# Expert and slot numbers held as bytes, and one register load for a round of eight tiles, in a two-layer tower on one core

## The chip, the cores and the metric

One NeuronCore of a Trainium2 chip runs the whole program. The metric is the device time of one execution in microseconds (us). Three executions of the kernel before are at hand. The engines are called as the profile calls them: PE (TensorE; PEld is its weight load), DVE (VectorE), ACT (ScalarE), POOL (GpSimd) and SP (SyncE, which issues DMAs). Each has its own sequencer, which goes through that engine's instructions in order and hands the work to the engine.

## The reference

The program is a tower of two layers over 8 x 500 tokens of width 128: embeddings, a state-space layer and a mixture of experts, then sparse attention and a second mixture of experts. The change touches only how the two mixtures find their weights. Per token and expert they compute

```
h = jax.nn.relu(xf @ W1e + b1e)
y = h @ W2e + b2e
acc = acc + cwe[:, None] * y        # cwe is zero but for the token's chosen experts
```

The first mixture has 8 experts with 512 hidden units and picks 2 of them per token. The second has 64 experts (8 groups of 8) with 256 hidden units and picks 4 per token.

## The kernel before

For each mixture f (0 and 1) the kernel sorts the token rows by expert, cuts the sorted rows into blocks of 128 and goes through *tiles*: a tile is one block with one expert that has rows in it. There are 70 tiles in loop 0 and 252 in loop 1, the most that the sorting can need, and the loops are written out: PE, DVE, ACT, POOL and SP each have a straight list of instructions in rounds of RING = 8 tiles. Which expert a tile belongs to, and which block, depends on the data, so it stands in tables that DVE writes (L1148 to L1170) and the sequencers of PE and DVE read into registers.

One tile works as follows, in the order of each engine's list:

- PE (`expert_tensor`, its inner `tiles` at L660): while blocks still come in, it turns the next block (L633, one matmul record). `first(u + 1, ...)` multiplies the next tile's block by W1 (L638, 8 records in loop 0, 4 in loop 1); the block's place in the ring of turned blocks comes from a register. `second(..., u)` multiplies the hidden values of this tile by W2 (L645, 8 records or 4); where the expert's W2 begins comes from a register. It waits for DVE's and ACT's part of the hidden values (L673, L674), and for W1 and the block of the next tile.
- DVE (`expert_vector`, its inner `tiles` at L579): copies the turned block out of PSUM (L554), does half of bias and relu (L559), and copies W1 of the tile three ahead from `big` into a ring of four (`stage`, L550); where W1 begins comes from a register. In loop 1, from tile 148 on, it adds one gathered result on three of four tiles (`combine_pick`, L1328).
- ACT does the other half of bias and relu (L605) and copies the results (L623). SP stores results, two tiles in one DMA.
- POOL gathers the sorted rows of each block with an indirect DMA (L867, 63 blocks in loop 0 and 126 in loop 1, in a ring of eight), and in loop 1 later gathers results (L874).

The registers are held by the class `Words` (L469). It has two words a tile for eight tiles, of which DVE uses the first. Four registers are filled by one register load (L478, TENSOR_LOAD in the trace): two tiles at a time, always for the same tiles of the *next* round, after every second tile:

```
second(words.value(u, 0), u)
if u % 2 and first_tile + u + RING < c.tiles:
    words.load(first_tile + RING, u - 1)
```

Before a loop, `Words` issues four such loads (L475), which fill the first eight tiles, on PE ahead of its first turn, and on DVE ahead of its first stage; DVE has one more for tiles 1 and 2 (`pairs_of`, L461). `value` (L481) reads a register into an address: FUSED_REGOPS in the trace, one instruction that holds several register operations; on PE `second` has another one for each further piece of W2 (L645). The tables hold 32-bit words that are already multiplied: (expert x columns of W1 or W2) and (place in the ring x 128). They are written by one-partition operations of DVE once per mixture: L1164 and L1165 the experts, L1166 and L1167 the places for DVE, L1169 and L1170 the places for PE.

Of the kernel before, what the change touches and what calls it, by code (L numbers as in the profile page):

```python
# [18 lines left out]
I32 = mybir.dt.int32  # L19
I16 = mybir.dt.int16  # L20
U32 = mybir.dt.uint32
ALU = mybir.AluOpType
# [3 lines left out]
D = 128  # L26
# [18 lines left out]
class Ffn:  # L45
# [25 lines left out]
    def blocks_for(self, tile):  # L71
# [15 lines left out]
TAB = FFN[1].tab  # L87
# [6 lines left out]
KEEP = {0: 32, 1: 67}  # L94
# [63 lines left out]
def tower_kernel(nc, a, out):  # L158
# [15 lines left out]
    with ExitStack() as ctx:  # L174
# [7 lines left out]
        def sb(name, shape, dt=F32):  # L182
            return ctx.enter_context(nc.sbuf_tensor(name, shape, dt))
# [78 lines left out]
        table = sb("table", [1, 2 * TAB], I32)  # L262
        w0 = 2 * FFN[0].tab
        assert 2 * w0 <= 2 * TAB <= 512
        tile_tables = [table[0:1, 0:w0], cst[0:1, 128:128 + 2 * TAB].bitcast(I32)]
        stage_tables = [table[0:1, w0:2 * w0], table[0:1, 0:2 * TAB]]
# [192 lines left out]
        def pairs_of(engine, table, tau, n, top_a, top_b):  # L459

            _, words = nc.values_load_multi_w_load_instructions(  # L461
                table[0:1, bass.ds(tau * 2, 2 * n)], engines=[engine], min_val=0, max_val=max(top_a, top_b),
                skip_runtime_bounds_check_because="the tables hold clipped numbers of experts and places in the ring")

            def within(word, top):
                return nc.s_assert_within(word, 0, top, skip_runtime_bounds_check_because="the tables hold clipped numbers")
            return [within(w, top_a) for w in words[0::2]], [within(w, top_b) for w in words[1::2]]

        class Words:  # L469

            def __init__(self, engine, p, table, first, top_a, top_b):
                self.engine, self.table, self.first, self.tops = engine, table, first, (top_a, top_b)
                self.regs = [engine.alloc_register(f"{p}word{n}") for n in range(2 * RING)]
                for u in range(0, RING, 2):
                    self.load(0, u)  # L475

            def load(self, first_tile, u):
                self.engine.reg_load(self.regs[2 * u:2 * u + 4], self.table[0:1, bass.ds((first_tile + (self.first + u)) * 2, 4)])  # L478

            def value(self, u, which):  # L480
                word = self.engine.snap(self.regs[2 * u + which], min_val=0, max_val=max(self.tops))  # L481
                return nc.s_assert_within(word, 0, self.tops[which], skip_runtime_bounds_check_because="the tables hold clipped numbers")
# [59 lines left out]
        def expert_vector(dve, c, combine_pick):  # L542
# [6 lines left out]
            def stage(w1, u):  # L549
                v.tensor_copy(ring.w1[u % U], w1v[:, bass.ds(w1, c.wcols)]).then_inc(S(p + "w1_ready"), 1)  # L550
# [15 lines left out]
            w1, _ = pairs_of(mybir.EngineType.DVE, stage_tables[c.n], 0, 2, (c.E - 1) * c.wcols, (KEEP[c.n] - 1) * 128)  # L566
            words = Words(dve, p, stage_tables[c.n], 2, (c.E - 1) * c.wcols, (KEEP[c.n] - 1) * 128)
# [4 lines left out]
            stage(w1[0], 1)  # L572
            dve.wait_ge(S(p + "turned"), 2)
            v.tensor_copy(ring.blocks[:, 128:256], ps[:, 1, 0:128]).then_inc(S(p + "blocks_in"), 1)
            stage(w1[1], 2)
# [3 lines left out]
            def tiles(first_tile, count):  # L579
                for u in range(count):  # L580
                    if first_tile + u in c.turn_at:
                        n = c.turn_at[first_tile + u]
                        dve.wait_ge(S(p + "turned"), n + 1)
                        turn(n)
                    dve.wait_ge(S(p + "hid_filled"), first_tile + (u + 4))
                    rectify(u + 1)
                    stage(words.value(u, 0), u + 3)
                    if u % 2 and first_tile + u + RING < c.tiles:
                        words.load(first_tile + RING, u - 1)
                    n = first_tile + u - COMBINE_AT  # L590
                    if c.n and n >= 0 and n % COMBINE_STEP:
                        combine_pick(n - n // COMBINE_STEP - 1)
# [35 lines left out]
        def expert_tensor(pe, c):  # L628
# [20 lines left out]
            words = Words(pe, p, tile_tables[c.n], 0, (c.E - 1) * c.HC * D, (KEEP[c.n] - 1) * 128)  # L649
# [295 lines left out]
        def _(dve):  # L945
# [45 lines left out]
            def route(c, me, dve):  # L991
# [162 lines left out]
                keep = KEEP[f]  # L1154
                numbers = tileno[0:1, 0:tab]
                tiles_, stages_ = (t_.rearrange("o (t w) -> o t w", w=2) for t_ in (tile_tables[f], stage_tables[f]))
                if f:
                    me.did(TT(out=block, in0=numbers, in1=one, op=ALU.subtract))
# [3 lines left out]
                else:  # L1162
                    me.did(TT(out=block, in0=numbers, in1=one, op=ALU.subtract))
# [1136 lines left out]
```

## Time and profile before

| | |
|---|---|
| three executions | 1136.02, 1134.34, 1134.40 us; median 1134.4 |
| profiled execution, first to last instruction (span) | 1221.9 us |
| profiled execution's own time | the profile gives no other than its span |
| loop 0 in the span | 257.7 to 393 us |
| loop 1 in the span | 793.1 to 1142 us |
| instructions recorded | 18019 |

A row of the trace gives the start in us from the beginning of the span, the duration, the engine, the line of the kernel and the operation. An engine with a q behind its name (PEldq, DVEq) is that engine's sequencer. The profiled execution is 87.5 us longer than the median.

### The profile page before, as it was taken

The page shows a single profiled execution, that of the slowest core. Times are in us where ns is not written, and L with a number is a line of the kernel's source. Part 1 is how long each engine was busy: PE and PEld are TensorE (multiplying, and loading weights), DVE is VectorE, ACT ScalarE, POOL GpSimd, SP SyncE. Part 2 cuts the span into 40 slices and gives each one's busy share as a digit, 9 for nine tenths or more (in the row PEclk, how much of TensorE's full clock was granted, in tenths as well). Part 3 has the DMA queues.
Part 4 walks back from the last instruction along what each step waited for, and adds up shares of the span by engine and source line. Part 5 has one row for each costly group of instructions (what it writes and reads, how often), then busy time and mean ns, then how long its engine had stood idle before and what let it go on. Part 6 is the DMA issues. An engine that isn't in the chain of part 4 may idle for free.

```text
span 1221.9 us, 18019 instructions
## 1 busy us (share of the span) xinstructions
PE 802.4 (66%) x5133; PEld 637.8 (52%) x5133; DVE 778.2 (64%) x2305; ACT 437.9 (36%) x1233; POOL 510.6 (42%) x528
## 2 busy tenths in 40 slices
PE   0218963879998248778587511287887897888343
PEld 0105552679998124434255401177776787777332
DVE  7885467656665248888766699855555555666642
ACT  2543241524444134443103304533343444444200
POOL 7841001255540634662101002466664435555574
PEclk9759965579999556666665555599999998999755
DMA  2290089012221287566400404133332223333222
GB/s 69 76 403 37 1 249 309 1 50 70 71 66 38 60 143 140 118 143 131 77 1 1 132 0 127 33 85 85 89 83 81 83 77 87 88 96 94 59 72 75
DMA packets 116599, 112.95 MB, mean 92 GB/s; under 512 B 16403, under 2 KB 102994, under 8 KB 116258
## 3 DMA queue, kind: packets, MB, share of 16 engines
q1 hardware_dynamic: 103228, 84.68, 25.3%
q0 software_dynamic: 13280, 27.13, 8.2%
q8 instruction: 49, 0.80, 0.3%
q14 instruction: 42, 0.34, 0.1%
HBM read 76.15 MB, written 35.57 MB: 91 GB/s over the span
## 4 chain that ended last, share of the span: by engine, by line
PE 55%; DVE 22%; issue 9%; POOL 5%; ACT 4%; DMA 3%; another core or an unknown queue 1%; SPq 0%; DVEq 0%; POOLq 0%; ACTq 0%
PE ps L638 18%; PE ps L645 15%; DVE wide L1348 6%; PE ps L1969 4%; POOL wide L810 3%; PE ps L633 3%; DVE wide L1229 3%; PE ps L2231 3%; PE ps L2139 2%; PE ps L2180 2%; ACT wide L1757 2%; DVE bnst L955 2%; POOL wide L874 1%; PE ps L2076 1%; PE ps L2224 1%
## 5 line engine op out<-in xcount | busy, mean ns | idle before, releaser
L645 PE MATMUL ps<-big,wide 128*128 x1568 | 238.1, 282 | 33.9 <-ACT wide L605 20.6
L638 PE MATMUL ps<-wide 128*128 (+1 forms) x1580 | 247.1, 287 | 18.9 <-DVE wide L554 12.2
L867 POOL DMA_INDIRECT wide<-xrows,holder x189 | 182.8, 967 | 158.1 <-PE ps L633 116.1
L559 DVE TENSOR_SCALAR wide<-ps,wide 128x128 f32<-128x128 f32 x395 | 131.7, 348 | 156.9 <-PE ps L638 138.4
L638 PEld LDWEIGHTS ps<-wide 128*128 128x128 f32 x1580 | 206.2, 195 | 40.8 <-issue 32.9
L645 PEld LDWEIGHTS ps<-big,wide 128*128 128x128 f32 x1568 | 203.7, 194 | 44.5 <-issue 43.9
L605 ACT ACTIVATE wide<-ps,wide 128x128 f32<-128x128 f32 x395 | 137.8, 367 | 202.4 <-PE ps L638 184.9
L1348 DVE TENSOR_REDUCE wide<-ps 125x3 f32<-125x1500 f32 (+1 forms) x96 | 143.7, 1540 | 46.7 <-PE ps L1969 45.3
L874 POOL DMA_INDIRECT wide<-results,place x128 | 127.6, 997 | 100.1 <-DVE h L1328 44.0
L1969 PE MATMUL ps<-big 97*125 97x500 bf16 x256 | 104.8, 545 | 40.3 <-DVE wide L1348 32.5
L623 ACT COPY wide<-ps 128x128 f32<-128x128 f32 x322 | 85.2, 264 | 92.1 <-PE ps L645 78.1
L550 DVE COPY wide<-big 128x258 f32 (+2 forms) x328 | 107.4, 327 | 3.9 <-issue 3.8
L856 POOL TENSOR_SCALAR wide<-tileno,sm 125x128 f16<-125x128 f16 x36 | 23.5, 653 | 172.2 <-DVE sm L1210 143.0
L1969 PEld LDWEIGHTS ps<-big 97*125 97x125 bf16 x256 | 42.6, 191 | 89.5 <-DVE wide L1348 50.8
L901 POOL DMA_INDIRECT wide<-results,place x64 | 60.9, 952 | 60.4 <-SPq L540 34.3
L554 DVE COPY wide<-ps 128x128 f32<-128x128 f32 x185 | 53.7, 290 | 41.5 <-PE ps L633 33.5
L1328 DVE SCALAR_TENSOR_TENSOR h<-wide,gate,h 125x128 f32<-125x128 f32 x128 | 43.2, 350 | 28.7 <-DMA wide<-results,place 23.4
L2248 PE MATMUL ps<-wide 125*128 125x79 f16 (+2 forms) x192 | 22.1, 262 | 54.6 <-DVE wide L1229 49.7
L633 PE MATMUL ps<-cst,wide 128*128 128x128 f32 x189 | 53.7, 287 | 5.5 <-issue 5.2
L1757 ACT ACTIVATE wide<-h,shift,rs 125x128 f32<-125x128 f32 x112 | 45.2, 483 | 25.6 <-DVE shift L972 19.4
L2119 PE MATMUL ps<-cst,wide 125*128 125x125 f32 x96 | 20.9, 370 | 48.6 <-ACT wide L1757 48.4
L2231 PE MATMUL ps<-b,cst 8*125 8x128 f32 (+1 forms) x128 | 33.0, 435 | 24.8 <-issue 20.6
(388 smaller groups left out, 1102.7 us busy)
## 6 DMA issues: line engine op xcount, KB each, us to landing
results<-wide SPq DMA_DIRECT2D x161, 128.0 KB, 1.8
big<-kappa SPq DMA_DIRECT2D x8, 1750.0 KB, 21.0
big<-parts SPq DMA_DIRECT2D x96, 125.0 KB
big<-in_L_ffn_W_dram SPq DMA_DIRECT2D x10, 1024.0 KB, 9.4
big<-in_L_ffn_W_dram SPq DMA_DIRECT2D x64, 128.0 KB, 2.6
parts<-wide SPq DMA_DIRECT2D x24, 250.0 KB
xrows<-wide SPq DMA_DIRECT2D x2, 1792.0 KB
wide<-results,place POOLq DMA_INDIRECT x192
```

The lines of the kernel that those rows point to most:

```text
L550: v.tensor_copy(ring.w1[u % U], w1v[:, bass.ds(w1, c.wcols)]).then_inc(S(p + "w1_ready"), 1)
L559: last = v.tensor_scalar(ring.hid[u % 2][:, 128 * k:128 * k + 128], ps[:, 4 + u % 2, 128 * k:128 * k + 128], w[:, hid + k:hid + k + 1], 0. ...
L605: last = s.activation(ring.hid[u % 2][:, 128 * k:128 * k + 128], ps[:, 2 + u % 2, 128 * k:128 * k + 128], ACT.Relu, bias=w[:, hid + k:hid ...
L623: s.copy(ring.res[u], ps[:, 6 + u % 2, 0:D]).then_inc(S(p + "res_ready"), 1)
L633: t.transpose(ps[:, u % 2, 0:128], ring.rows[u % RING], ident).then_inc(S(p + "turned"), 1)
L638: last = t.matmul(ps[:, (2 if k < c.HC // 2 else 4) + u % 2, 128 * k:128 * k + 128], ring.w1[u % U][:, 128 * k:128 * k + 128], turned, sta ...
L645: last = t.matmul(ps[:, 6 + u % 2, 0:D], ring.hid[u % 2][:, 128 * k:128 * k + 128], w[:, D * k:D * k + D], start=k == 0, stop=k == c.HC - 1)
L867: gp.indirect_dma_start(ring.rows[j % RING], None, xrows[:, :], bass.IndirectOffsetOnAxis(ap=holder[:, j:j + 1], axis=0)).then_inc(S(f"row ...
L874: gp.indirect_dma_start(ring.rows[n % 8], None, results[1 if n < FIRST_PICKS else 2][:, :], bass.IndirectOffsetOnAxis(ap=place[f][:, k, t: ...
L1348: v.tensor_reduce(out=mcol[:, j, H * b + lo:H * b + hi], in_=ps[0:R, 3 * (n % 2):3 * (n % 2) + hi - lo, 0:L], axis=AX.X, op=ALU.max).then_ ...
L1969: last = t.matmul(ps[0:R, 3 * (n % 2) + head - lo, 0:L], stack[0:SROWS, 0, b % 2, head, R * j:R * j + R], stack[0:SROWS, 1, b % 2, head, : ...
L2231: last = t.matmul(p[0:R, D * j:D * j + D], cT[0:c.E, R * j:R * j + R], b2[0:c.E, f, :], start=True, stop=True)
```

## The change

The tables become bytes (U8) that hold the expert's number and the block's place themselves. `value` multiplies by the size of a step when the address is made. PE loads sixteen words (eight tiles x two) with one instruction at the head of each round, DVE eight words (eight tiles x one), likewise. The loads before the loops go away, but for one of eight words on DVE that serves tiles 1 and 2. DVE's table holds only the expert, already shifted by three tiles.

```
-        table = sb("table", [1, 2 * TAB], I32)
+        table = sb("table", [1, 4 * TAB], U8)
         w0 = 2 * FFN[0].tab
-        assert 2 * w0 <= 2 * TAB <= 512
-        tile_tables = [table[0:1, 0:w0], cst[0:1, 128:128 + 2 * TAB].bitcast(I32)]
-        stage_tables = [table[0:1, w0:2 * w0], table[0:1, 0:2 * TAB]]
+        assert w0 % 16 == 0 and w0 + FFN[0].tab <= TAB
+        tile_tables = [table[0:1, 0:w0], table[0:1, TAB:3 * TAB]]
+        stage_tables = [table[0:1, w0:w0 + FFN[0].tab], table[0:1, 3 * TAB:4 * TAB]]
...
         class Words:
-            def __init__(self, engine, p, table, first, top_a, top_b):
-                self.engine, self.table, self.first, self.tops = engine, table, first, (top_a, top_b)
-                self.regs = [engine.alloc_register(f"{p}word{n}") for n in range(2 * RING)]
-                for u in range(0, RING, 2):
-                    self.load(0, u)
-            def load(self, first_tile, u):
-                self.engine.reg_load(self.regs[2 * u:2 * u + 4], self.table[0:1, bass.ds((first_tile + (self.first + u)) * 2, 4)])
+            def __init__(self, engine, p, count, tops):
+                self.engine, self.tops = engine, tops
+                self.regs = [engine.alloc_register(f"{p}word{n}") for n in range(count)]
+            def load(self, row, at_, count):
+                self.engine.reg_load(self.regs[0:count], row[0:1, at_:at_ + count])
+            def value(self, n, which, scale):
+                word = self.engine.snap(self.regs[n], min_val=0, max_val=max(self.tops))
...
+                return word * scale
...
(DVE, before the loop)
-            w1, _ = pairs_of(mybir.EngineType.DVE, stage_tables[c.n], 0, 2, ...
-            words = Words(dve, p, stage_tables[c.n], 2, ...
+            words = Words(dve, p, RING, (c.E - 1, KEEP[c.n] - 1))
+            words.load(tile_tables[c.n], 0, RING)
...
(DVE, a round)
             def tiles(first_tile, count):
+                words.load(stage_tables[c.n], first_tile, count)
...
-                    stage(words.value(u, 0), u + 3)
-                    if u % 2 and first_tile + u + RING < c.tiles:
-                        words.load(first_tile + RING, u - 1)
+                    stage(words.value(u, 0, c.wcols), u + 3)
...
(PE, a round)
             def tiles(first_tile, count):
+                words.load(tile_tables[c.n], 2 * first_tile, 2 * count)
...
-                    first(u + 1, words.value(u, 1))
+                    first(u + 1, words.value(2 * u + 1, 1, 128))
...
-                    second(words.value(u, 0), u)
-                    if u % 2 and first_tile + u + RING < c.tiles:
-                        words.load(first_tile + RING, u - 1)
+                    second(words.value(2 * u, 0, c.HC * D), u)
...
(the tables)
-                me.did(TS(tiles_[:, :, 0], one, float(c.HC * D), None, ALU.mult))
-                me.did(TS(stages_[:, 0:tab - 1, 0], one[:, 1:tab], float(c.wcols), None, ALU.mult))
-                me.then(TS(wrap, numbers, float(keep), -128.0 * keep, ALU.is_ge, ALU.mult))
-                me.did(v.scalar_tensor_tensor(stages_[:, :, 1], numbers, 128.0, wrap, ALU.mult, ALU.add))
+                me.did(v.tensor_copy(tiles_[:, :, 0], one))
+                me.did(v.tensor_copy(stage_tables[f][:, 0:tab - 3], one[:, 3:tab]))
                 me.settle()
-                me.then(TS(wrap, block, float(keep), -128.0 * keep, ALU.is_ge, ALU.mult))
-                me.then(v.scalar_tensor_tensor(tiles_[:, 0:tab - 1, 1], block[:, 1:tab], 128.0, wrap[:, 1:tab], ALU.mult, ALU.add))
+                me.then(TS(wrap, block, keep, -keep, ALU.is_ge, ALU.mult))
+                me.then(TT(out=tiles_[:, 0:tab - 1, 1], in0=block[:, 1:tab], in1=wrap[:, 1:tab], op=ALU.add))
```

## Rows read from the trace of the kernel before

**Rows 1.** Page, busy time of the engines and the chain that ended last, by line.

```profile
PE 802.4 (66%) x5133; PEld 637.8 (52%) x5133; DVE 778.2 (64%) x2305; ACT 437.9 (36%) x1233; POOL 510.6 (42%) x528
...
PE ps L638 18%; PE ps L645 15%; DVE wide L1348 6%; PE ps L1969 4%; POOL wide L810 3%; PE ps L633 3%; DVE wide L1229 3%; PE ps L2231 3%; PE ps L2139 2%; PE ps L2180 2%; ACT wide L1757 2%; DVE bnst L955 2%; POOL wide L874 1%; PE ps L2076 1%; PE ps L2224 1%
```

**Rows 2.** Register loads (L478) by engine and table: ns min/median/max, first to last start.

```profile
L478 DVEq TENSOR_LOAD <-table x161: 336/343/493, 255.0 to 1133.0; - x161
L478 PEldq TENSOR_LOAD <-cst x126: 327/333/616, 790.4 to 1132.6; - x126
```

**Rows 3.** PE in order of time in loop 0: start, duration, last column idle before.

```profile
302.65 0.27 PE L633 MATMUL ps<-cst,wide 128*128 128x128 f32 x1
...
304.55 0.27 PE L633 MATMUL ps<-cst,wide 128*128 128x128 f32 x1
```

**Rows 4.** Sequencer of PE, 301 to 303: register load, and the next wait behind it.

```profile
L478 PEldq TENSOR_LOAD <-table x1: 329/329/329, 301.4 to 301.4; - x1
...
L667 PEldq EVENT_SEMAPHORE  x1: 51/51/51, 301.8 to 301.8; - x1
```

**Rows 5.** PE in order of time in loop 1, while POOL gathers nothing.

```profile
990.94 0.71 PE L638 MATMUL ps<-wide 128*128 x4
...
997.58 0.71 PE L638 MATMUL ps<-wide 128*128 x4
...
998.57 0.61 PE L638 MATMUL ps<-wide 128*128 x4
...
999.70 0.71 PE L638 MATMUL ps<-wide 128*128 x4
```

**Rows 6.** Register operations: DVE's in loop 0 and loop 1, then PE's of L645.

```profile
L481 DVEq FUSED_REGOPS  x70: 67/67/80, 261.7 to 392.0; - x70
...
L481 DVEq FUSED_REGOPS  x252: 55/55/70, 795.5 to 1141.3; - x126
...
L645 PEldq FUSED_REGOPS  x462: 46/52/52, 260.7 to 1141.1; - x154
```

**Rows 7.** Busy us (x instructions) by stretch of loop 1, granted clock, DMA share, GB/s.

```profile
799.00:911.00 112.00, 92.62 (x665) 80.12 (x664) 58.92 (x222) 43.57 (x148) 72.01 (x74) 0.98 0.31 87
990.00:1006.00 16.00, 15.86 (x126) 14.47 (x124) 9.56 (x35) 9.08 (x29) 2.76 (x3) 1.00 0.25 70
```

**Rows 8.** POOL, DVE and PE in order of time around one pause in loop 1.

```profile
867.59 1.06 POOL L867 DMA_INDIRECT wide<-xrows,holder  x1 [0.31 <-issue]
868.96 0.94 POOL L867 DMA_INDIRECT wide<-xrows,holder  x1 [0.30 <-issue]
...
870.64 0.29 DVE L554 COPY wide<-ps 128x128 f32<-128x128 f32 x1 [1.63 <-PE ps L633]
...
868.69 0.27 PE L633 MATMUL ps<-cst,wide 128*128 128x128 f32 x1
...
871.08 0.37 PE L638 MATMUL ps<-wide 128*128 x1 [1.05 <-DVE wide L554]
```

**Rows 9.** The chain that ended last, 788 to 795: the start of loop 1.

```profile
790.63 0.34 DVEq L461
...
791.00 0.34 DVEq L478
...
792.50 0.21 DVE wide L550
```

**Rows 10.** Start of loop 0: PE's first turn, DVE's first stage.

```profile
256.76 0.66 PE L633 MATMUL ps<-cst,wide 128*128 128x128 f32 x2 [2.66 <-issue]
...
256.51 0.43 DVE L550 COPY wide<-big 128x516 f32<-128x516 f32 x1 [1.71 <-issue]
```

**Rows 11.** DVE's L1166 of mixture 1 and of mixture 0, then both L1167.

```profile
L1166 DVE TENSOR_SCALAR wide<-tileno 1x256 f32<-1x256 f16 x1 | 0.3, 276 | 0.0
...
L1166 DVE TENSOR_SCALAR wide<-tileno 1x80 f32<-1x80 f16 x1 | 0.2, 180 | 0.0
...
L1167 DVE SCALAR_TENSOR_TENSOR table<-tileno,wide x2: 231/322/413, 201.8 to 733.9; 1x80 int32<-1x80 f16 x1, 1x256 int32<-1x256 f16 x1
```

More of the change, by code:

```diff
@@ L21 @@
 U32 = mybir.dt.uint32
+U8 = mybir.dt.uint8
 ALU = mybir.AluOpType
@@ L457, in weight_loads @@
             return c.E // (8 if c.n else 4) + (W2_EARLY if c.n else 8)
[L459 to L467, printed above, removed]
-        class Words:
-            def __init__(self, engine, p, table, first, top_a, top_b):
-                self.engine, self.table, self.first, self.tops = engine, table, first, (top_a, top_b)
-                self.regs = [engine.alloc_register(f"{p}word{n}") for n in range(2 * RING)]
-                for u in range(0, RING, 2):
-                    self.load(0, u)
-            def load(self, first_tile, u):
-                self.engine.reg_load(self.regs[2 * u:2 * u + 4], self.table[0:1, bass.ds((first_tile + (self.first + u)) * 2, 4)])
-            def value(self, u, which):
-                word = self.engine.snap(self.regs[2 * u + which], min_val=0, max_val=max(self.tops))
-                return nc.s_assert_within(word, 0, self.tops[which], skip_runtime_bounds_check_because="the tables hold clipped numbers")
+        class Words:
+            def __init__(self, engine, p, count, tops):
[5 more added lines that the diff above has]
+                word = self.engine.snap(self.regs[n], min_val=0, max_val=max(self.tops))
+                word = nc.s_assert_within(word, 0, self.tops[which], skip_runtime_bounds_check_because="the tables hold clipped numbers")
+                return word * scale
             def free(self):
@@ L565, in expert_vector @@
             dve.wait_ge(S(f"w{c.n}_ld"), 16 * weight_loads(c))
-            w1, _ = pairs_of(mybir.EngineType.DVE, stage_tables[c.n], 0, 2, (c.E - 1) * c.wcols, (KEEP[c.n] - 1) * 128)
-            words = Words(dve, p, stage_tables[c.n], 2, (c.E - 1) * c.wcols, (KEEP[c.n] - 1) * 128)
+            words = Words(dve, p, RING, (c.E - 1, KEEP[c.n] - 1))
+            words.load(tile_tables[c.n], 0, RING)
             dve.wait_ge(S("bank_filled"), nfill[at[f"holder{c.n}", len(c.parts) - 1]])
@@ L571, in expert_vector @@
             v.tensor_copy(ring.blocks[:, 0:128], ps[:, 0, 0:128]).then_inc(S(p + "blocks_in"), 1)
-            stage(w1[0], 1)
+            stage(words.value(2, 0, c.wcols), 1)
             dve.wait_ge(S(p + "turned"), 2)
             v.tensor_copy(ring.blocks[:, 128:256], ps[:, 1, 0:128]).then_inc(S(p + "blocks_in"), 1)
-            stage(w1[1], 2)
+            stage(words.value(4, 0, c.wcols), 2)
             dve.wait_ge(S(p + "hid_filled"), 3)
@@ L647, in second @@
                 last.then_inc(S(p + "res_filled"), 1)
-            words = Words(pe, p, tile_tables[c.n], 0, (c.E - 1) * c.HC * D, (KEEP[c.n] - 1) * 128)
+            words = Words(pe, p, 2 * RING, (c.E - 1, KEEP[c.n] - 1))
             pe.sem_inc(S(p + "hid_filled"), 2)
@@ L1152, in route @@
                 dve.wait_ge(S("emptied_dve"), nth[at[f"expert{f}", 0]])
-                keep = KEEP[f]
+                keep = float(KEEP[f])
                 numbers = tileno[0:1, 0:tab]
-                tiles_, stages_ = (t_.rearrange("o (t w) -> o t w", w=2) for t_ in (tile_tables[f], stage_tables[f]))
+                tiles_ = tile_tables[f].rearrange("o (t w) -> o t w", w=2)
+                me.did(TT(out=block, in0=numbers, in1=one, op=ALU.subtract))
                 if f:
-                    me.did(TT(out=block, in0=numbers, in1=one, op=ALU.subtract))
                     me.then(TS(second, one, float(c.E), None, ALU.is_ge))
@@ L1161, in route @@
                     me.then(v.scalar_tensor_tensor(one, second, -float(c.E), one, ALU.mult, ALU.add))
-                else:
-                    me.did(TT(out=block, in0=numbers, in1=one, op=ALU.subtract))
-                me.did(TS(tiles_[:, :, 0], one, float(c.HC * D), None, ALU.mult))
-                me.did(TS(stages_[:, 0:tab - 1, 0], one[:, 1:tab], float(c.wcols), None, ALU.mult))
-                me.then(TS(wrap, numbers, float(keep), -128.0 * keep, ALU.is_ge, ALU.mult))
-                me.did(v.scalar_tensor_tensor(stages_[:, :, 1], numbers, 128.0, wrap, ALU.mult, ALU.add))
+                me.did(v.tensor_copy(tiles_[:, :, 0], one))
+                me.did(v.tensor_copy(stage_tables[f][:, 0:tab - 3], one[:, 3:tab]))
                 me.settle()
-                me.then(TS(wrap, block, float(keep), -128.0 * keep, ALU.is_ge, ALU.mult))
-                me.then(v.scalar_tensor_tensor(tiles_[:, 0:tab - 1, 1], block[:, 1:tab], 128.0, wrap[:, 1:tab], ALU.mult, ALU.add))
+                me.then(TS(wrap, block, keep, -keep, ALU.is_ge, ALU.mult))
+                me.then(TT(out=tiles_[:, 0:tab - 1, 1], in0=block[:, 1:tab], in1=wrap[:, 1:tab], op=ALU.add))
                 S_ = m["slot"]
```

## Prediction

> **What bounds the kernel now.** The page comes first. No engine is busy for more than 66% of the span, and the chain that ended last lies by 36% on PE's lines of the two expert loops, L638, L645 and L633 [rows 1]. So loop 0 (135 us) and loop 1 (349 us) are paced by PE, or by what makes PE wait, and the change acts there, since it takes register loads off two sequencers. Next the loads themselves: 161 on DVE and 161 on PE (126 of them in loop 1), and two of L461, a third of a microsecond each [rows 2], four words each. None of them shows as busy time, so the question is whether PE or DVE ever run dry behind one.
>
> In loop 0 they don't. A tile with a turn is 17 matmul records and takes 1.90 us from turn to turn, which is 0.112 us a record without a hole [rows 3]. The load starts at 301.4, the sequencer is at the next wait at 301.8, and the next turn's matmul starts at 302.65 [rows 3, 4]: the sequencer is 0.85 us ahead after the load. The 31 loads within the loop cost nothing there, covered by that lead.
>
> In loop 1 a tile is half as long, and the lead is gone. Between 990 and 1000 POOL is nearly idle and the clock is 1.00 [rows 7], so nothing else disturbs. Two tiles without a turn, from 997.58 to 999.70, are 16 records, 1.79 us at 0.112 each, and take 2.12: one load in them costs 0.33 us, its own length. The eight tiles from 990.94 to 999.70 hold four loads and five turns (L633, the first at 991.93 and the last at 997.35), 69 records or 7.71 us, and take 8.76: 1.05 us, **0.26 us a load** [rows 5]. This is the number on which the forecast rests.
>
> Elsewhere in loop 1 there are pauses of another kind. In the stretch 799 to 911 PE is busy for 92.6 of 112 us [rows 7]. PE's turn starts at 868.69 and DVE's copy of it only at 870.64, after 1.63 us of idleness; then PE's L638 waits 1.05 us for DVE. Meanwhile POOL is in the second of two gathers back to back [rows 8]. No load of PE or DVE explains that pause, so the change does not end it.
>
> **The change part by part.** The sum is made on the profiled execution, of which only the span of 1221.9 us is known. It is 87.5 us longer than the median of 1134.4, and the trace does not say where, so I take the difference in us over to the median.
>
> (a) Before the loops. In loop 1 DVE goes through five loads from 790.63 on, 0.37 us apart, and its first stage follows at 792.50; these loads lie on the chain [rows 9]. Four go away: 1.5 us. PE's four before its first turn go too, and its first load now stands behind first(0), covered by that and by the wait for W1. Loop 0 begins in the same way: PE idles 2.66 us ahead of its turn and DVE 1.71 ahead of its stage, both put down to issue [rows 10]. 1.5 us again. Together **-3.0** (0 if the rows gathered by POOL are late instead, 3.5 at most).
>
> (b) The tables. L1166 and L1167 go away, one-partition operations of 0.28 + 0.41 us and 0.18 + 0.23 us [rows 11]. L1164, L1165 and L1170 become simpler at the same size. DVE's list is in order and everything of the sorting follows in it: **-1.1**.
>
> (c) Register operations. One multiplication joins each. The DVE ones hold one operation more in loop 0 (they add where W1 begins) and take 67 ns in place of 55 [rows 6]: 12 ns. Three in a tile on PE are 36 ns, which matter only right behind a load, where the sequencer has no lead: 32 rounds, 1.2 us. The other end is that they always count, 252 x 0.036 = 9 us. I take **+1** since the pair 998.57 to 999.70 shows the hole only at the load.
>
> (d) The length of the new load. The trace has no load of sixteen words. The low end is 0.33 us [rows 2], since it moves the same 16 bytes as a load of four 32-bit words does now. The high end is the price by the word, 0.333 / 4 = 0.083 us, so 1.33 us. Nearest is the load that moves as many bytes. I add the twelve further registers at 17 ns each, what L645's instruction takes for each of its three register operations (52 ns) [rows 6]: 0.53 us. DVE's eight words are 0.41 us in the same way.
>
> (e) Loop 1, PE. Before: 122 loads within the loop at 0.26 us, 32 us. After: 32 loads, each 0.20 us longer and wholly exposed for the excess, 0.46 us, 15 us. Gain 17 us, if all of it counts. In the first 77 tiles each tile needs one gather, whose spacing back to back is 1.37 us [rows 8]; a bare PE tile with a turn is 9 records, 1.01 us. There POOL would take PE's place, and I count nothing for them, 77 of 252. That leaves 17 x 0.69 = 12 us, with nothing taken for (c): **-12**.
>
> (f) Loop 0, PE: nine loads, 0.20 longer, against a lead of 0.85 us: 0. DVE: it is busy for 59 of 112 us [rows 7] and waits for PE in the rest, so 0.41 for 0.34 stays covered. If that cover went, 41 x 0.07 = 3 us.
>
> Where the stall goes, POOL's gathers are late next. The sum is -3.0 - 1.1 + 1 - 12 = -15, so **1119 us**. With 0.33 us a load and all tiles counting it is 122 x 0.26 - 32 x 0.26 = 23 and 4 more, 1107. The forecast's own range is 1107 to 1128.
>
> **The rivals.** *POOL or the pauses take it all back.* If the pauses of 1 to 1.6 us depend on POOL's rhythm and not on PE's, PE only arrives earlier at the same pause. Only the 16 us between 990 and 1006 gain, 1 us, with (a) and (b): 1129. For it: POOL is busy 72 of 112 us with 74 gathers [rows 7]. Against: that leaves it free for a third of the stretch.
>
> *The load is priced by its words* (slower). At 1.33 us, 32 loads cost 0.26 + 1.0 each, 40 us in place of 32, loop 0 gives (1.0 - 0.85) x 9 = 1, and with (a) and (b) the time is 1134.4 + 8 + 1 - 4 = 1139 to 1140. It decides from a load of 1.19 us on, where 32 x (x - 0.07) reaches 32 + 4. Against it: nothing in these rows, as all loads have four words; for the forecast only the equal bytes. If each word were a trip of its own at 0.33 us, 5.3 us a load would cost 32 x 5.2 - 32 in loop 1 and 9 x 4.1 in loop 0: some +170, 1300.
> The Trainium skill, page "Runtime: NRT & Kernel Launch", section "Instruction fetch mechanics", states such a rule: about 200 ns a register even for many, for loads from HBM. By it four words would take 0.8 us, where the trace has 0.33, so it disagrees here; by it an estimate for sixteen is 3.2 us, and the sum would be about 1215.
>
> *DVE's loads.* Every load of before starts at a multiple of 16 bytes; every second one of DVE now starts 8 bytes beyond one. If those go word by word at 0.34, 2.7 us, DVE is late by that less the idle time of two tiles, 0.7 us each (53 us over 77 tiles [rows 7]), 16 times: 1119 + 21 = 1140.
>
> *The multiplication becomes an instruction of its own*: 0.1 us of PE's sequencer for each of two values, 252 x 0.2 = 50 us at most, 6 at least (32 rounds). At about a third, it cancels the gain: 1134.
>
> **How the numbers follow.** Forecast 0.50, POOL 0.16, words 0.13, a trip a word (the page's price with it) 0.06, DVE 0.08, multiplication 0.07. A measurement tells 0.2% (2.3 us) from no change. Faster: 0.50 + 0.16 = 0.66. Same: 0.07. Slower: 0.13 + 0.06 + 0.08 = 0.27. The predicted time is the forecast's, 1119. The range goes from 1106 to 1141, and leaves out the trip a word and the ends of the others.
>
> **What would show it.** TENSOR_LOAD of sixteen words at about 0.5 us, 41 on PE and 43 on DVE. Between 990 and 1000, seven of eight tiles at 0.112 us a record and one hole a round. The first stage of loop 1 within 1 us of the last holder copy. Loop 0 still at 1.90 us a tile. Loop 1 shorter by 10 to 17 us. A load over 1.2 us, holes behind DVE's odd loads, or POOL back to back in the first 77 tiles would prove the forecast wrong.

## The result, and the profile after

The changed kernel takes **1312.8 us** (median of 4 runs, 1308.6 to 1323.2) where the kernel before takes 1135.2 beside it (4 runs, 1134.3 to 1139.8). The ratio is 1.156, with a 95% interval from 1.151 to 1.161: slower by 178 us, where 15 us of gain were forecast, and outside the range.

The page of the changed kernel's profiled execution (1312.3 us), whose busy row stands against [rows 1]:

```profile
span 1310.5 us, 17777 instructions
PE 829.0 (63%) x5133; PEld 688.3 (53%) x5133; DVE 782.7 (60%) x2301; ACT 448.4 (34%) x1233; POOL 507.2 (39%) x528
PEclk9759855589989657667655555888888877887955
PE 51%; DVE 23%; issue 13%; DMA 5%; POOL 4%; ACT 2%; DVEq 1%; SPq 0%; ACTq 0%; POOLq 0%
```

The same 5133 matmuls, and 178 us more, with no instruction more for any engine to run (PE's busy time is longer all the same: 829.0 us, where a second execution of the kernel before, shown below, has 787.5). "issue" on the chain is time in which an engine waited for nothing that the profile shows, 13% or 170 us. The waits of PE in the changed kernel (engine, line, what it waited for: us in total, times, longest) say where:

```profile
PE ps L622 <- issue: 86.3, 26, 3.7
PE ps L627 <- issue: 54.0, 15, 3.9
```

26 + 15 = 41 waits, one for each register load on PE, 140 us together. PE's own queue is what keeps it. The register loads by engine and table (ns min/median/max, first to last start), which stand against [rows 2], and the register operations against [rows 6]:

```profile
L467 DVEq TENSOR_LOAD <-table x43: 952/2080/2141, 254.7 to 1230.9; - x43
L467 PEldq TENSOR_LOAD <-table x41: 2174/4042/4232, 257.7 to 1230.5; - x41
...
L470 PEldq FUSED_REGOPS  x644: 58/63/68, 262.1 to 1236.0; - x161
L470 DVEq FUSED_REGOPS  x326: 67/67/84, 256.9 to 1236.4; - x163
```

**A load of sixteen bytes takes 4.04 us**, not 0.53, and VectorE's load of eight takes 2.08; PE's last load, of eight, takes 2.17, VectorE's last, of four, 0.95. That is 0.25 us for each element. The multiplication is no instruction of its own.

PE in order of time in loop 1 of the changed kernel (start, duration, last column idle time before it), the stretch that answers to [rows 5]:

```profile
869.12 0.61 PE L634 MATMUL ps<-big,wide 128*128 x4
873.39 0.42 PE L622 MATMUL ps<-cst,wide 128*128 128x128 f32 x1 [3.67 <-issue]
873.66 1.22 PE L627 MATMUL ps<-wide 128*128 x4
874.67 1.06 PE L634 MATMUL ps<-big,wide 128*128 x4
875.52 0.42 PE L622 MATMUL ps<-cst,wide 128*128 128x128 f32 x1
875.74 1.06 PE L627 MATMUL ps<-wide 128*128 x4
876.59 0.74 PE L634 MATMUL ps<-big,wide 128*128 x4
877.17 0.27 PE L622 MATMUL ps<-cst,wide 128*128 128x128 f32 x1
877.28 0.61 PE L627 MATMUL ps<-wide 128*128 x4
```

Two losses in each round of eight tiles. One is the hole: 3.67 us in which PE has nothing. The other was in no step of mine: behind the hole, four matmuls take 1.06 us in place of 0.61 and a turn 0.42 in place of 0.27, until 877.2. These are the rows of a matmul at the lower clock, 1.2 GHz. The granted clock of the two stretches, the two tiles behind the hole and the rest of the round (same columns as [rows 7], the clock before the DMA share):

```profile
873.40:876.80 3.40, 3.40 (x15) 3.26 (x16) 1.13 (x4) 0.64 (x2) 1.43 (x2) 0.51 0.05 11
877.20:886.80 9.60, 6.14 (x56) 5.95 (x53) 5.26 (x19) 4.08 (x14) 5.73 (x7) 1.00 0.38 105
```

PE idles in the hole, and the two tiles behind it (three in the later rounds of the loop) run at half the clock. From the first matmul of one tile to that of the next, the round's tiles take 5.00, 2.08 and 1.56 us (medians of the first 77), and the other five 1.00. The windows of the changed kernel (busy us by engine, then granted clock, DMA share, GB/s) against [rows 7]:

```profile
815.00:911.00 96.00, 70.91 (x507) 68.28 (x506) 47.68 (x169) 35.91 (x113) 51.90 (x55) 0.86 0.28 76
1055.00:1237.00 182.00, 130.00 (x906) 127.21 (x904) 84.48 (x307) 71.76 (x227) 76.21 (x80) 0.82 0.26 71
```

Loop 0 has the same hole, and the lead of 0.85 us takes only about as much of it: in the middle rounds the tile with the hole takes 4.98 us in place of 1.90, and the two tiles behind it 2.83 and 2.23, since they too run in part at the lower clock. PE in order of time there, which answers to [rows 3]:

```profile
302.05 0.30 PE L622 MATMUL ps<-cst,wide 128*128 128x128 f32 x1 [2.74 <-issue]
302.34 1.15 PE L627 MATMUL ps<-wide 128*128 x8
303.33 1.83 PE L634 MATMUL ps<-big,wide 128*128 x8
```

The profile that the prediction read spans 1221.9 us, far above the kernel's own time. The sum needs one that is nearer, a second profiled execution of the kernel before:

> The kernel before, unchanged, for a profile whose span is near its own time. The profile that the prediction read spans 1221.9 us where its timed runs take 1134 to 1140. Expected of this one: span 1133 to 1140 us. Theory A (what a load costs is its trips): TensorE's 4-word loads in the loops near 0.33 us each, and the hole that each leaves between two tiles under the 0.26 us that the prediction read, nearer the 0.16 us that the kernel without loads in its loops gives (19 us over 122 + 31 loads, some of them hidden). Rival: the holes are 0.26 us here too and the kernel without loads gained less than they hold because something else becomes late; then the tiles without a load in that kernel are slower than the tiles without a load here.

It took 1134.4 us, with a span of 1132.7, just below what was expected. Its page, its loads, and two stretches of loop 1:

```profile
span 1132.7 us, 18019 instructions
PE 787.5 (70%) x5133; PEld 636.5 (56%) x5133; DVE 788.3 (70%) x2305; ACT 448.2 (40%) x1233; POOL 508.0 (45%) x528
...
L478 PEldq TENSOR_LOAD <-cst x126: 327/333/338, 776.0 to 1050.6; - x126
...
779.00:871.00 92.00, 89.56 (x696) 83.08 (x696) 66.59 (x233) 48.67 (x154) 69.46 (x74) 0.98 0.40 107
871.00:933.00 62.00, 61.66 (x491) 56.98 (x490) 43.62 (x154) 35.50 (x113) 41.72 (x45) 1.00 0.40 109
```

From the first L638 of a loop to its last, loop 0 took 133.2 us and loop 1 279.3. The changed kernel took 169.9 and 421.8: +36.7 and +142.5, 179 of the 178 us between the two executions (outside the loops it is 1 us shorter). In the execution that the prediction read, loop 1 took 347.9 us, which is 69 of the 89 us by which its span is longer than this one: the long pauses of [rows 8] and the 92.6 busy of 112 us in [rows 7] belong mostly to that execution. Here PE is busy for 89.6 of 92 us in the first 77 tiles. Why that one was slower stays open.

### The profile page after: what moved, and what is told of

The parts are those of the page before. It is cut to its first block, busy times and chain, and to the rows that moved or that the text cites. A ratio compares the mean times of both kernels' runs of the same rounds, so it can differ in the third digit from the quotient of the medians.

```text
span 1310.5 us, 17777 instructions
## 1 busy us (share of the span) xinstructions
PE 829.0 (63%) x5133; PEld 688.3 (53%) x5133; DVE 782.7 (60%) x2301; ACT 448.4 (34%) x1233; POOL 507.2 (39%) x528
## 4 chain that ended last, share of the span: by engine, by line
PE 51%; DVE 23%; issue 13%; DMA 5%; POOL 4%; ACT 2%; DVEq 1%; SPq 0%; ACTq 0%; POOLq 0%
PE ps L627 17%; PE ps L634 15%; DVE wide L1332 6%; PE ps L1953 3%; DVE wide L1213 2%; POOL wide L862 2%; PE ps L622 2%; PE ps L2123 2%; PE ps L2164 2%; DMA wide<-results,place 2%; DVE bnst L943 2%; ACT wide L1741 1%; PE ps L2215 1%; PE ps L2103 1%; POOL wide L798 1%
## 5 line engine op out<-in xcount | busy, mean ns | idle before, releaser
L627 PE MATMUL ps<-wide 128*128 (+1 forms) x1580 | 270.1, 308 | 57.6 <-issue 54.0
L627 PEld LDWEIGHTS ps<-wide 128*128 128x128 f32 x1580 | 236.3, 219 | 65.4 <-issue 60.1
L855 POOL DMA_INDIRECT wide<-xrows,holder x189 | 180.1, 953 | 221.8 <-PE ps L622 185.0
L634 PE MATMUL ps<-big,wide 128*128 x1568 | 259.8, 301 | 0.0
L634 PEld LDWEIGHTS ps<-big,wide 128*128 128x128 f32 x1568 | 232.5, 218 | 0.0
L622 PE MATMUL ps<-cst,wide 128*128 128x128 f32 x189 | 56.6, 302 | 87.9 <-issue 86.3
L622 PEld LDWEIGHTS ps<-cst,wide 128*128 128x128 f32 x189 | 29.2, 156 | 92.8 <-issue 92.8
```

The lines of the kernel that those rows point to most:

```text
L622: t.transpose(ps[:, u % 2, 0:128], ring.rows[u % RING], ident).then_inc(S(p + "turned"), 1)
L627: last = t.matmul(ps[:, (2 if k < c.HC // 2 else 4) + u % 2, 128 * k:128 * k + 128], ring.w1[u % U][:, 128 * k:128 * k + 128], turned, sta ...
L634: last = t.matmul(ps[:, 6 + u % 2, 0:D], ring.hid[u % 2][:, 128 * k:128 * k + 128], w[:, D * k:D * k + D], start=k == 0, stop=k == c.HC - 1)
L855: gp.indirect_dma_start(ring.rows[j % RING], None, xrows[:, :], bass.IndirectOffsetOnAxis(ap=holder[:, j:j + 1], axis=0)).then_inc(S(f"row ...
```

## The experiments

**Theory A**: a register load makes one trip to memory for each element, except that four 32-bit words at a 16-byte boundary go in one trip. (The trace shows how long a load takes, and no trips; "trip" is the name here for the step in which the length grows.) **B**: the time goes with the bytes, or with the tiles that a load serves. **B'**: with the number of registers. **C**: it is the place, the head of a round, where nothing is prefetched. Times are medians; ratios are against the kernel before on the same chip.

**1. The same bytes, loaded as words.**

```
-self.engine.reg_load(self.regs[0:count], row[0:1, at_:at_ + count])
+n = -(-count // 4)
+self.engine.reg_load(self.regs[0:n], row[0:1, at_:at_ + 4 * n].bitcast(I32))
...
+word = (word >> (8 * (n % 4))) & 255
```

> Same byte tables and same places as the changed kernel, but the load takes the sixteen (DVE: eight) bytes as four (two) 32-bit words, and the register operation shifts and masks the byte out. Theory A (a load makes one trip of about 0.25 us for each byte element, but one trip for 16 bytes of 32-bit words): the loads take 0.33 us like those of before; loop 1 loses 122 holes of 0.26 us and gets 32, so 1135 - 3 - 1 - 24 and some 2 us for the longer register operations: 1109 us. Theory B (the length goes with the bytes or tiles served, whatever the element): 4 us a load, about 1312. Theory C (it is the place at the head of the round that costs): above 1250.

1154.7 us, ratio 1.016 [1.012, 1.019]. Its loads:

```profile
L468 DVEq TENSOR_LOAD <-table x43: 319/529/790, 254.7 to 1075.4; - x43
L468 PEldq TENSOR_LOAD <-table x41: 327/332/776, 256.4 to 1075.0; - x41
```

The same sixteen bytes at the same places take 0.33 us as four words and 4.04 as sixteen elements. B and C fall: neither bytes nor place changed. The load is as theory A says; the time of 1109 us that I expected with it is missed by 46. VectorE's two words (8 bytes) take 0.53, more than four words do, so fewer than four go singly. The kernel is still 17 us slower than the one before, because shift and mask aren't free: PE has 1589 fused register instructions in place of 1106, and 644 single ones (ALU_OP) and 161 moves besides. Among the first 77 tiles of loop 1 those without a load take 1.14 to 1.20 us in place of 1.00, and loop 1 takes 302.3 us.

**2. Sixteen registers of 32-bit words**, the change's shape with the tables in the type of before.

```
-table = sb("table", [1, 4 * TAB], U8)
+table = sb("table", [1, 2 * TAB], I32)
```

> The changed kernel with tables of 32-bit elements; PE's load fills the same sixteen registers from 64 bytes, DVE's eight from 32. Theory A: 64 bytes are four trips, 4 x 0.2465 + 0.09 = 1.07 us a load; 32 loads with holes of 1.0 us in loop 1 against 122 of 0.26: 1135 - 4 + 0 = 1131 us. Theory B' (the length goes with the number of registers, as my forecast's rival had it): 4 us a load, 1312. Theory C: above 1250.

1137.6 us, ratio 1.000 [0.998, 1.002]. Its loads on PE, and the hole of one round (PE in order of time):

```profile
L467 PEldq TENSOR_LOAD <-cst x32: 676/1191/1275, 779.5 to 1057.3; - x32
...
883.93 0.61 PE L634 MATMUL ps<-big,wide 128*128 x4
885.24 0.30 PE L622 MATMUL ps<-cst,wide 128*128 128x128 f32 x1 [0.70 <-issue]
885.48 0.71 PE L627 MATMUL ps<-wide 128*128 x4
```

Sixteen registers, four times the bytes, less than a third of the time: B' falls too. Four trips are 1.19 us and the last load of eight words, two trips, is 0.68. A round has one tile of 2.06 us, one of 1.10 and most others at 0.89 to 1.00; the granted clock of loop 1 is 0.99, as in the kernel before. That is the kernel that my forecast described, without its price of 0.53 us, and it gains nothing: 6.6 us more than the 1131 that theory A gave. Its starts are 2.9 us shorter and its tables 1.0, and its loops 2.0 and 2.6 us longer (135.2 and 281.9 us).

**3. Bytes, but in the places of before**: four registers behind every second tile, for the tile pair eight further on.

```
+for u in range(0, RING, 2):
+    words.load(tile_tables[c.n], 2 * u, 4, 2 * u)
...
-words.load(tile_tables[c.n], 2 * first_tile, 2 * count)
...
+if u % 2 and first_tile + u + RING < c.tiles:
+    words.load(tile_tables[c.n], 2 * (first_tile + RING + u - 1), 4, 2 * (u - 1))
```

> Byte tables, but PE loads four registers at a time for the next round, after every second tile, as before the change; DVE as changed. Theory A: four byte elements are four trips, 1.07 us; 122 holes of 1.0 us in loop 1 in place of 0.26: +90, less 4, plus what DVE's 2.08 us loads add: 1220 to 1240 us. If the count of registers or the head of the round is the cause, 0.33 us a load and 1131 to 1145.

1235.2 us, ratio 1.086 [1.082, 1.091]. Its loads, and the window of loop 1:

```profile
L467 PEldq TENSOR_LOAD <-table x161: 982/987/1173, 257.4 to 1151.2; - x161
...
789.00:1159.00 370.00, 287.86 (x2134) 253.01 (x2134) 191.49 (x702) 158.63 (x502) 186.47 (x198) 1.00 0.29 80
```

The count of registers and the places are those of before; only the element is a byte, and 0.33 becomes 0.99. It costs 98 us. A round's loads add up to the same 4 us as in the changed kernel, yet it is 78 us faster: the clock of loop 1 stays at 1.00, and in loop 0, where the lead is 0.85 us, it hides most of a 1 us load (138.2 us against 169.9).

**4. No loads within the loops.** The kernel before with the loads of its loops taken out; it leaves out the expert numbers of all but the first eight tiles.

```
 second(words.value(u, 0), u)
-if u % 2 and first_tile + u + RING < c.tiles:
-    words.load(first_tile + RING, u - 1)
...
-first(u + 1, words.value(u, 1))
+first(u + 1, (words.value(u, 1) & 0) + at_)
```

> The kernel before without the register loads within the loops: the registers keep the numbers of the first eight tiles, so most tiles use a wrong expert; the place of the block is a constant added to a masked register. This prices the old loads by themselves. My step (e): 122 holes of 0.26 us go, less 1 for the longer register operations: 1104 us. If the pauses with POOL's gathers take the time back: 1133.

1118.8 us, ratio 0.983 [0.980, 0.987], between the 1104 of step (e) and the 1133 of its rival. All 153 loads on each engine are worth 19 us, 17.4 of them in loop 1 (261.9 us against 279.3); loop 0, at 133.6 against 133.2, gains nothing. By stretch, a tile of loop 1 takes 1.194 / 0.985 / 0.942 / 0.962 us here and 1.186 / 1.110 / 1.079 / 1.050 in the second execution of the kernel before (means; 77 tiles behind the first; 56 with few gathers; 15 with none; the last 103). Per load, of two tiles, the gain is nothing, 0.25, 0.27 and 0.18 us.

In the first 77 tiles the holes are there in the kernel before (two tiles are 1.15 + 1.10 us where two without a load are 2.00), but without them PE waits for gathered rows instead. Its waits for POOL's gathers (us in total, times, longest), here from 784 to 876 us and in the kernel before from 780 to 871:

```profile
PE ps L631 <- DMA wide<-xrows,holder: 8.0, 11, 1.5
...
PE ps L633 <- DMA wide<-xrows,holder: 2.3, 2, 1.9
```

So of the two views set down for the second profile of the kernel before, the rival was right there: the hole is as read, and something else becomes late.

**5. Which engine's loads cost the time?** The tables of one engine in bytes, those of the other in words.

```
+stable = sb("stable", [1, TAB], I32)
-stage_tables = [table[0:1, w0:w0 + FFN[0].tab], table[0:1, 3 * TAB:4 * TAB]]
+stage_tables = [stable[0:1, 0:FFN[0].tab], stable[0:1, 0:TAB]]
...
(the mirror)
-tile_tables = [table[0:1, 0:w0], table[0:1, TAB:3 * TAB]]
+ttable = sb("ttable", [1, w0], I32)
+tile_tables = [ttable[0:1, 0:w0], cst[0:1, 128:128 + 2 * TAB].bitcast(I32)]
```

> The changed kernel, with VectorE's table of stages kept as 32-bit words (8 registers, 32 bytes, two trips) and TensorE's table in bytes as changed. Theory A1 (TensorE's 4.04 us load sets the round, VectorE's 2.08 us lies beside it): the time stays near the changed kernel's, 1300 to 1313 us, and loop 1's last tile of eight stays at 5.0 us from start to start. Rival A2 (both add up, since VectorE's load delays the stages that TensorE waits for): a fall of 0.5 to 1.5 us a round over 43 rounds, 1250 to 1290 us.

> The mirror of the last: TensorE's table in 32-bit words (16 registers, 64 bytes, 1.17 us), VectorE's table of stages in bytes (8 registers, 2.08 us). Its partner with both in words took 1137.6 us. Theory A1: VectorE runs ahead of TensorE by more than 2 us in its stages, and nothing is added: 1137 to 1145 us. Rival A2: VectorE's 2.08 us holds TensorE in each round for 0.9 us more than now: 43 x 0.9 = 39 us, 1177 us.

Bytes on TensorE alone: 1316.4 us, ratio 1.158 [1.154, 1.161]. Bytes on VectorE alone: 1140.4 us, ratio 1.003 [1.001, 1.005], 3 us more than with words on both. The loads of the byte tables in each, and those of PE's words in loop 1 of the second:

```profile
L468 PEldq TENSOR_LOAD <-table x41: 2321/4074/4229, 254.4 to 1232.4; - x41
...
L468 DVEq TENSOR_LOAD <-table x41: 949/2075/2151, 260.2 to 1061.6; - x41
L468 PEldq TENSOR_LOAD <-cst x32: 644/1151/1272, 779.8 to 1061.3; - x32
```

TensorE's load is the whole of the loss (the 1316 is 3 us above what I expected, with an interval that holds the changed kernel's 1.156); VectorE's 2.08 us lie beside PE's work. A1 holds.

**6. Two numbers to a word.** 16-bit numbers, multiplied when the table is built, eight words a round on PE and four on VectorE.

```
-self.engine.reg_load(self.regs[0:count], row[0:1, at_:at_ + count])
+self.engine.reg_load(self.regs[0:count // 2], row[0:1, at_:at_ + count].bitcast(I32))
...
+word = word >> 16 if n % 2 else word & 65535
```

> The change's shape with other tables: 16-bit numbers, already multiplied by the width, two to a 32-bit word. TensorE loads 8 words at the top of each round (32 bytes at a 16-byte boundary, two trips), VectorE 4 words (one trip); a value is the word's upper or lower half, one shift or one mask in the instruction that held the multiplication. Theory A: TensorE's load takes 0.60 to 0.68 us where 16 words took 1.17, VectorE's 0.33; no instruction more than in the changed kernel; against the 16-word kernel (1137.6) 0.5 to 0.6 us less in each of 40 rounds, less what loop 0 hides: 1118 to 1126 us. Rival (halves as costly as bytes, because the shift or mask becomes an instruction of its own in front of each tile): 0.05 to 0.12 us more a tile over 322 tiles, 1140 to 1155 us, with more register instructions in TensorE's group of the value's line than the changed kernel's 644.

1138.1 us, ratio 1.002 [1.000, 1.003]. Its loads and the instructions of its values on PE:

```profile
L467 PEldq TENSOR_LOAD <-table x41: 335/590/831, 258.6 to 1057.3; - x41
...
L470 PEldq FUSED_REGOPS  x322: 75/79/82, 259.6 to 1060.6; - x161
L470 PEldq MOVE  x322: 29/29/33, 261.4 to 1061.2; - x161
...
L638 PEldq ALU_OP  x322: 32/32/42, 261.5 to 1061.3; - x161
```

The load is 0.59 us as theory A says, and the tile with the hole takes 1.62 us in place of 2.06. But the time did not fall, so my number of 1118 to 1126 was wrong. The rival's mechanism was right, though its 1140 to 1155 lies above the 1138.1: only the shift joins the fused instruction. The mask needs a MOVE and an ALU_OP in front, 322 times each. In the last 103 tiles of loop 1 the tiles without a load take up to 1.13 us in place of 0.89 to 0.93, and the mean of all is 1.076 us where experiment 2 has 1.055.

**7. Off the boundary by eight bytes**, and **eight bytes twice a round**: experiment 2 with loop 1's table of PE moved by two words, and experiment 3 with eight registers behind every fourth tile.

```
-tile_tables = [table[0:1, 0:w0], cst[0:1, 128:128 + 2 * TAB].bitcast(I32)]
+tile_tables = [table[0:1, 0:w0], table[0:1, 2:2 + 2 * TAB]]
...
(the second)
-    if u % 2 and first_tile + u + RING < c.tiles:
-        words.load(tile_tables[c.n], 2 * (first_tile + RING + u - 1), 4, 2 * (u - 1))
+    if u % 4 == 3 and first_tile + u + RING - 3 < c.tiles:
+        words.load(tile_tables[c.n], 2 * (first_tile + RING + u - 3), 8, 2 * (u - 3))
```

> The 16-word kernel (1137.6 us) with loop 1's table of TensorE moved by two words, so that each of its loads begins 8 bytes past a 16-byte boundary; loop 0's table stays at a boundary, as a control in the same run. Theory A as measured so far (only an aligned block of four 32-bit words goes in one trip, all else element by element at 0.25 us): loop 1's loads take 16 x 0.25 + 0.09 = 4.1 us, loop 0's stay at 1.17, the time is near the changed kernel's less what loop 0 lost there (1295 to 1312). Theory A' (a trip fetches what lies in one 16-byte block, wherever the load begins): five trips, 1.4 us, and 1140 to 1150 us. Theory A'' (the words before the first boundary and behind the last one singly, aligned blocks between them in one trip each): 2 + 3 + 2 = 7 trips, 1.9 us, 1160 to 1170 us.

> The changed kernel with its byte tables, TensorE's bytes fetched eight at a time behind every fourth tile for the tiles that use them next, where the changed kernel fetches sixteen at the top of each round (four at a time behind every second tile took 1235.2 us). The same bytes, so theory A alone (a hole for each load: its length, less the 0.19 us by which the queue runs ahead, plus 0.10 us in the tile behind it, no clock term) says 2 x 1.99 us a round against 4 x 0.89 in the kernel of four bytes: 0.42 us more in each of 32 rounds of loop 1, and as much in loop 0 less its cover: 1245 to 1255 us. With the clock term as I read it in the changed kernel (the granted clock falls to half after a hole of 3.7 us and the next tiles take 1.6 us more): if a hole of 1.9 us is enough for it, up to 2 x 1.6 us a round more, 1300 us and above, and the granted clock of loop 1 is under 0.9; if it isn't, the clock of loop 1 stays at 1.00 and the time is that of theory A.

The first took 1281.5 us, ratio 1.127 [1.124, 1.130], the second 1279.9, ratio 1.127 [1.121, 1.134]. The loads of the first in loop 0 and in loop 1, then those of the second and its loop 1:

```profile
L467 PEldq TENSOR_LOAD <-table x9: 850/1106/1293, 258.1 to 383.1; - x9
...
L467 PEldq TENSOR_LOAD <-table x31: 2190/4106/4198, 794.7 to 1199.5; - x31
```

```profile
L467 PEldq TENSOR_LOAD <-table x81: 1917/2110/2427, 254.8 to 1197.2; - x81
...
801.00:1206.00 405.00, 296.75 (x2135) 281.03 (x2135) 196.86 (x702) 158.76 (x502) 187.40 (x198) 0.91 0.27 73
```

Sixteen words 8 bytes past a boundary take 4.11 us, as long as sixteen bytes; at a boundary, in the same run, 1.11. The length of the load is as theory A says, and A' and A'' fall. The time is 14 us below the 1295 to 1312 that I gave for A: loop 0, whose loads stay short, takes 135.9 us in place of 169.9, more than I took off, and loop 1, at 425.5, is as slow as in the changed kernel (421.8). In the second kernel the clock is 0.91 in loop 1: after some of its 1.8 us holes the next tiles run at half the clock, after others not. So its 1279.9 lies between the 1245 to 1255 of holes alone and the 1300 of a drop behind each.

**8. The best of both?** Experiment 2 with PE's loads as before, four words behind every second tile, and the first four behind the first half of tile 0.

```
 first(0, 0)
+for u in range(0, RING, 2):
+    words.load(tile_tables[c.n], 2 * u, 4, 2 * u)
...
-words.load(tile_tables[c.n], 2 * first_tile, 2 * count)
...
+if u % 2 and first_tile + u + RING < c.tiles:
+    words.load(tile_tables[c.n], 2 * (first_tile + RING + u - 1), 4, 2 * (u - 1))
```

> The 16-word kernel (1137.6 us), with TensorE's loads back at four 32-bit words behind every second tile and its first four behind the first tile's first half instead of before the first turn; VectorE loads eight words at the top of a round, as there. So it keeps the shorter start and the smaller tables and gives up the one long load. By the traces of the kernel before and of the 16-word kernel: VectorE's first load to TensorE's first tile 2.51 to 1.28 us in loop 1 and 3.32 to 1.67 in loop 0 (2.9 less), the tables 1.0 less, the loops 281.9 + 135.2 back to 279.3 + 133.2, and 0.4 for four loads in a row behind the first half of tile 0. Theory A: 1136.9 - 2.9 - 1.0 + 0.4 = 1133.4 us, 0.3% faster than before, TensorE's loads 0.33 us each. Rival (what the start gains, the rows gathered by GpSimd take back in the first 77 tiles of loop 1): within 0.1% of before, 1136 to 1138.

1136.5 us, ratio 1.000 [0.998, 1.001], 12 runs. I expected 1133.4, and the interval leaves that out; the number is the rival's, 1136 to 1138. Its profiled execution (1131.9) has the shorter starts, but loop 1 takes 283.3 us in place of 279.3. About 1.7 of the 4 us are put down to the multiplications: a tile behind a load takes 1.144 us in place of 1.130 (medians behind the first 77 tiles), 122 times. Another 0.7 are the four loads in a row (1.91 us from tile 0 to tile 1 in place of 1.20). Most of the rest lies in the first 77 tiles (1.209 for 1.186 us each), among pauses that differ between the two executions; what ends them was not followed up. No version was found that beats the kernel before.

## Why the prediction was wrong

**(d) failed, and everything with it.** I took 0.53 us for the load of sixteen, "nearest is the load that moves as many bytes", plus 17 ns for each further register. Bytes are not what a load pays for. Its length grows in steps of 0.25 to 0.33 us, one for each element, or one for each block of four 32-bit words where the load starts at a 16-byte boundary. All register loads of the kernel before that I used as rows were of the one form that goes in a single trip, so 0.33 us was the price of one trip and not of four registers or sixteen bytes. The change left that form: the number of bytes stayed, the number of trips went from one to sixteen, and 4.04 us is three times the high end that I gave for (d), 1.33. Even with words, at 1.19 us, the forecast of 1119 would have been too low by 18 us (experiment 2).

**The rival "a trip a word" was right for bytes**, with 0.06. (For words it is wrong, as [rows 2] show: four of them take 0.33 us in all. That the size of the element decides was in no rival.) It said 5.3 us a load and 1300 us; the load measured 4.04, and the time is 1313. That these are so near is partly luck: two errors nearly cancel. Its load was too long, because a trip behind the first is shorter than a load of one: 41 x 1.3 us too much. And it lacks the clock: behind each hole two tiles run at 1.2 GHz, 2.08 + 1.56 us where experiment 2 has 1.10 + 1.00, so 1.54 us a round, 48 us over 31 rounds, and by the tiles of loop 0 some 10 us more there. Of the 78 us between experiment 3 and the changed kernel, 51 are of loop 1 and 32 of loop 0, where the lead hides most of the short loads; 5 go back, since experiment 3 starts its loops later. The rule of the Trainium skill that stood beside it (page "Runtime: NRT & Kernel Launch", section "Instruction fetch mechanics", some 200 ns a register even in bulk, from HBM) is near to what bytes in SBUF show, 250 ns, and far from what aligned words show, 83 ns. Its 3.2 us was the better guide to the changed kernel than my row, though the sum by it, 1215, is 98 us too low as well, and I discarded it because the row disagreed.

**The rival of the words' price**, 1.33 us and 1139 to 1140, is right for another kernel than the change: experiment 2 has 1.19 us a load and 1137.6. Its decision point, 1.19 us, is right too: there, the ratio is 1.000.

**(e) was right on the old loads.** A load less gains 0.25 and 0.27 us in the two quiet stretches, as I read it from [rows 5], and nothing in the first 77 tiles, as I assumed. What was off is the last 103 tiles, where it gains 0.18. So 122 loads hold 17 us and not 32 x 0.69 = 22. And a new hole costs its length, less a lead of 0.1 to 0.2 us, plus 0.10 us in the tile behind it, a term that I didn't have; where it is 3.7 us long, the clock of the tiles behind it comes on top.

**(f) failed with (d)**: that the lead of 0.85 us covers the old loads is confirmed by experiment 4, but it doesn't cover 4.04 us. Nine loads cost 36.7 us. For VectorE (f) was right: even its 2.08 us stay covered (experiment 5).

**(a) holds for words, not for bytes.** From VectorE's first load to PE's first L638 the kernel before takes 3.32 and 2.51 us (loop 0, loop 1), experiment 2 takes 1.67 and 1.28, together 2.9 less, against 3.0. In the changed kernel it is 3.00 and 2.51, since its one load takes 2 us: 0.3.

**(b) holds.** From L1151's first operation on the tables to the first behind them: 1.62 and 3.80 us before, 1.25 and 3.15 after, 1.0 us less against 1.1.

**(c) holds**: 63 ns in place of 53 on PE, 67 in place of 55 on VectorE. Tiles of experiment 2 without a load are as short as those of experiment 4, so it counts only right behind a load.

**The other rivals.** *DVE's loads*: every second one is off a 16-byte boundary, and it makes no difference for bytes (2.08 us in the median, 2.14 at most); the fear was right for words (experiment 7). *The multiplication* stayed within the fused instruction. *POOL takes it back* was not tested by the change; experiment 4 shows it for the first 77 tiles, where waits for gathered rows grow from 2.3 to 8.0 us.

## What to carry to other kernels

What a register load costs here goes with its elements, not its bytes: load 32-bit words, in fours, from a 16-byte boundary, and check the boundary of every table. Packing numbers smaller shortened the load (0.59 us for 1.19) but saved no time, since the mask that unpacks them costs two more instructions on a sequencer that has little lead; unpacking by a shift alone was not tried. Where the sequencer has a lead (0.85 us in loop 0), short loads spread over the loop hide behind it, and one load of 4 us doesn't; where the hole is 3.7 us long, the TensorE clock is lost as well. And when a row's duration is to be scaled, ask first which of its properties the change keeps.

## What the runs showed of the hardware that I had not expected

- Register loads from SBUF in these runs (medians): four aligned 32-bit words 0.33 us, eight 0.59 to 0.68, sixteen 1.11 to 1.19; two words 0.53; four bytes 0.99, eight 2.08 to 2.11, sixteen 4.04; sixteen words 8 bytes past a boundary 4.11.
- A stall of PE's own queue of 3.7 us is followed by two or three tiles at half the clock (0.82 to 0.87 by stretch of loop 1); stalls of 1.8 us are so now and then (0.91 over the loop), and with those of 0.7 us in experiments 2 and 3 loop 1 stays at 0.99 and 1.00.
- The first matmuls behind a hole: a tile takes 1.10 us in place of 1.00 after a load of 0.33, 0.99, 1.19 or 2.11 us, at the full clock.
